# Delaying the side work of the first pass over a dense matrix by four steps: a four-layer graph network kernel on one Trainium2 core

## The chip, the cores and the metric

The kernel runs on one core of a Trainium2 chip (trn2). The metric is device time in microseconds (us) for one execution of the whole program, all four layers; lower is better. Matmuls and transposes run on TensorE (PE in the rows, PEld its weight loads), elementwise work and reductions on VectorE (DVE), activations on ScalarE (ACT), and there are GpSimd (POOL) and the queue of SyncE (SP), which issues most of the transfers.

## The reference

`x` is 8192x128, `adj` a dense 8192x8192 fp32 array that is mostly zeros. Every layer starts from `h = relu(layernorm(x))` and ends in `x = x + layer(h, adj)`.

```
# layer 0: weighted mean over neighbours, then a linear map
x = x + relu((inv_deg[:, None] * A_prime @ h) @ W0.T + b0)     # A_prime = alpha*adj, diagonal + (1-alpha)
# layer 1: a product W1 in hyperbolic space, a mean over adj, and a map back
XW = mobius_matvec(W1, h)
x = x + expmap0(relu(logmap0(... adj @ (gamma * XW) / (adj @ (gamma - 1)) ...)))
# layer 2: maximum over the 32 largest entries of each row of adj
x = x + max over topk(adj, 32) of (h @ W2.T + b2)
# layer 3: as layer 1 with a normalised adj + I, a product W3 and a bias
```

Layer 1 needs, for every row of `x` that layer 0 has finished, the layer norm, the clip, the product with `W1`, several norms, a logarithm and a tanh. This is called the preparation of the next layer below.

## The kernel before

The program is written engine by engine, each with its own loops; semaphores tie them together. Its stages are:

- **The start** (to about 59 us of the trace). `x` is loaded and normalised, and multiplied by `W0` ahead of the sums.
- **The first pass** (about 59 to 1476 us). `adj` is read once from HBM as 256 pieces of 1 MB. A piece is 512 rows by 512 columns; 16 pieces in a row (32 pairs of column tiles) make a group of 512 rows, and there are 16 groups, numbered 0 to 15. Each pair K (two per piece, 512 in all) goes through all engines: TensorE transposes it (`turn_pair`, L655) and multiplies the pair before it into the sums (`add_pair`, L667); ScalarE copies the transposed pair out of PSUM (`copy_pair`, L903) and makes a mask of the piece (`mask`, L910); GpSimd multiplies the mask by column numbers (L498); VectorE takes the eight largest of each row (L1473), for the top 32 of layer 2. SyncE stores the transposed pair back to HBM (L427) and loads the next piece (L436). ScalarE has four buffers for copies, which a stored pair frees (L902 waits), and a ring of three pieces of masks: `mask(K)` waits until VectorE has scanned pair K-6.
- **The turned pass** (about 1477 to 2465 us) reads the transposed matrix for layer 1 (L751), with the gathers of layer 2 beside it.
- **The rest** is layer 3, a second reading of the transposed matrix (L783), and the ends of all rows.

**The side work.** When a group's sums are complete, VectorE finishes its rows of `x` (`update`, L1360 to L1374) and sorts its candidates (`pick`, L1269 to L1354). Both are Python generators: VectorE's loop calls `next` on them twice after each piece, one call being a step, so that their instructions are spread between the scans. The preparation of the next layer is a third generator, on ScalarE and on VectorE (`prepare` on each), started at groups 3, 6, 9 and 12 for the three groups of rows before (`PREPS`), and once more behind the pass for the last four groups. ScalarE's generator makes one step per pair, VectorE's two per piece. So step s of both falls on pair s counted from the group at which the preparation began; step 32 is the first of the next group, step 95 the last of the third.

The preparation's handovers, in order:

1. VectorE centres the rows (L1389 at step 5; L1391 and L1392 at step 6) and tells ScalarE (`tell_act`, a semaphore). ScalarE waits for that at step 10 (`pause(10)`, then `wait_job`), squares two tiles per step (L929, six steps), and takes roots (L939).
2. VectorE waits for the roots at step 19, clips and scales (L1396, L1397). ScalarE waits for that at step 25 and squares again, one tile per step. TensorE turns a unit of four tiles at steps 26, 38 and 50 (L679), ScalarE copies it (L950), TensorE multiplies it by `W1` five steps after each turn (L687), and VectorE copies the product out at steps 32, 44 and 56 (L1404).
3. ScalarE squares the products (step 69), takes roots (L962, step 75), a logarithm (step 82) and a tanh (step 90); VectorE works on the small results at steps 77, 84, 85, 92 and 93. The last two are L1438 to L1444 and L1446 to L1449.

`pause(n)` yields n times. A waiting engine waits with everything behind it in its own order: if ScalarE waits in `wait_job`, the copies of the next pairs stand behind it, and TensorE needs them.

At a group's start SyncE holds the load of the group's fifth piece until VectorE has scanned the first pair of the group (L435), and the stores of the group's next pairs stand behind it in its queue:

```
                    if (n - SLOTS) % NPC == 0:
                        sp.wait_ge(scanned, 2 * (n - SLOTS) + 1)
                sp.dma_start(pieces[n % SLOTS], ...)
```

Of the kernel before, what the change touches and what calls it, by code (L numbers as in the profile page):

```python
# [75 lines left out]
def build(nc, x, adj, alpha, w0, b0, w1, w2, b2, w3, b3, out):  # L76
# [5 lines left out]
    NP = NT // 2  # L82
# [8 lines left out]
    LATE = 6  # L91
    PREPS = [(0, 3), (3, 6), (6, 9), (9, 12), (12, 16)]
    UNIT_GAP = 12
    EARLY = 6
    PARTS = [(0, 3), (3, 6), (6, 8)]
    DONE = [(0, 16), (16, 32), (32, 48), (48, 56), (56, 64)]
# [22 lines left out]
    with ctx:  # L119
# [267 lines left out]
        def pause(count):  # L387
            for _ in range(count):
                yield
# [221 lines left out]
        def _(pe):  # L611
# [79 lines left out]
            def adjacency_pass():  # L691
                pe.wait_ge(h0_copied, NG)
                turn_pair(0)
                pe.wait_ge(h0_taken, NG)
                for K in range(PAIRS):
                    if K + 1 < PAIRS:
                        turn_pair(K + 1)
                    add_pair(K)
                    for b, (first, end) in enumerate(PREPS[:-1]):
                        turned_from = end * NP + 20 + 2 * (end - first)  # L700
                        for u in range(first, end):
                            if K == turned_from + UNIT_GAP * (u - first):
                                turn_h1(u, b)
                            if K == turned_from + UNIT_GAP * (u - first) + 5:
                                project_h1(u, b)
# [96 lines left out]
            def turn_out(u):  # L802
                pe.wait_ge(out_scaled, u // SGG + 1)
                if u < EARLY:
                    into = psX[:, :]
# [9 lines left out]
            def project_out(u):  # L815
                pe.wait_ge(pj_copied, 2 * UNITS + u + 1)
                into = psY[:, :] if u < EARLY else halves[u % 2]
                if u < EARLY:
                    pe.wait_ge(out_taken, u)
                elif u >= EARLY + 2:  # L820
                    pe.wait_ge(out_taken, u - 1)
# [5 lines left out]
            def last_chunk():  # L827
                i, par = CHUNKS // 2 - 1, 1
                pe.wait_ge(tiles_made, CHUNKS * CT)
                for s in range(NSG):  # L830
                    pe.wait_ge(sums_added, (CHUNKS - 1) * NSG + s + 1)
                    for kk in range(2):
# [4 lines left out]
                        if turn >= 0:  # L837
                            turn_out(turn)
                project_out(EARLY - 1)
                turn_out(EARLY)  # L840
                for u in range(EARLY, NG):
# [13 lines left out]
        def _(act):  # L855
# [3 lines left out]
            def wait_job():  # L859
                asked[0] += 1  # L860
                act.wait_ge(for_act, asked[0])

            def job(out, in_, func, **kw):
                wait_job()
                nc.scalar.activation(out, in_, func, **kw).then_inc(from_act, 1)
# [58 lines left out]
            def prepare(first, end):  # L924
                tiles = range(first * TPG, end * TPG)
                ts = slice(first * TPG, end * TPG)

                def square(row, t):
                    st.mark(nc.scalar.activation(junk_tile, G[:, t, :], ACT.Square, accum_out=sm[:, row, t:t + 1]))  # L929
                    st.settle()  # L930

                yield from pause(10)
                wait_job()
                for t in tiles:
                    square(0, t)
                    if t % 2:
                        yield
                st.settle()
                nc.scalar.activation(sm[:, 1, ts], sm[:, 0, ts], ACT.Sqrt, scale=1.0 / P, bias=eps_col[:, :])\  # L939
                    .then_inc(from_act, 1)  # L940
                yield from pause(9)
                wait_job()
                for t in tiles:
                    square(2, t)
                    if t % TPG == TPG - 1:
                        u = t // TPG
                        act.wait_ge(pj_turned, u + 1)
                        if u >= 2:
                            act.wait_ge(pj_out, u - 1)
                        nc.scalar.activation(HT[:, u % 2, :], psX[:, :], ACT.Copy).then_inc(pj_copied, 1)  # L950
                        if end < NG:
                            yield from pause(UNIT_GAP - TPG)
                    yield
                st.settle(tell=from_act)
                yield from pause(8)
                wait_job()
                for t in tiles:
                    square(3, t)
                    if t % 2:
                        yield  # L960
                st.settle()
                nc.scalar.activation(sm[:, 7:9, ts], sm[:, 2:4, ts], ACT.Sqrt).then_inc(from_act, 1)  # L962
                yield from pause(7)
                job(sm[:, 13, ts], sm[:, 12, ts], ACT.Ln)
                yield from pause(8)
                job(sm[:, 5, ts], sm[:, 5, ts], ACT.Tanh)
# [212 lines left out]
        def _(dve):  # L1179
# [197 lines left out]
            def prepare(first, end):  # L1377
                ts = slice(first * TPG, end * TPG)
                n = (end - first) * TPG
# [11 lines left out]
                link(v.tensor_scalar(T(0), T(0), -1.0 / P, None, ALU.mult))  # L1391
                link(v.tensor_tensor(G[:, ts, :], X[:, ts, :], by_row(T(0), n), ALU.add))  # L1392
                tell_act()
                yield from pause(n // 2 + 7)
                answered()
                link(v.reciprocal(T(1), U(1)))  # L1396
                link(v.scalar_tensor_tensor(G[:, ts, :], G[:, ts, :], 0.0, by_row(T(1), n), ALU.max, ALU.mult),  # L1397
# [4 lines left out]
                for u in range(first, end):  # L1402
                    dve.wait_ge(pj_out, u + 1)
                    v.tensor_copy(G[:, u * TPG:(u + 1) * TPG, :], ps[:, :].rearrange("p (r f) -> p r f", f=P))\  # L1404
                        .then_inc(pj_taken, 1)
                    yield from pause(UNIT_GAP if u + 1 < end else 4)
                answered()
                dve.wait_ge(pj_taken, end)
                tell_act()
                yield from pause(n // 2 + 11)  # L1410
                answered()
                y, ys, q, y2, m = T(5), U(1), T(11), U(10), U(9)
                link(v.tensor_scalar(rows[:, 2:4, :], sm[:, 7:9, ts], 1e-15, None, ALU.max))
# [670 lines left out]
```

## Time and profile before

| what | value |
|---|---|
| time, median of 3 runs | 3695.63 us (3692.3 to 3698.97) |
| span of the profiled execution | 3738.5 us |
| first pass, from the first to the last product | 59 to 1476 us |
| TensorE busy | 3378.0 us, 90% of the span |
| VectorE busy | 2622.0 us, 70% |
| GpSimd busy | 2592.6 us, 69% |
| ScalarE busy | 1607.0 us, 43% |
| mean granted TensorE clock | 0.963 |

The page gives for the profiled execution its span only, no time of its own; the span is 42.9 us above the median of the timed runs. Columns of a timeline row are the start, the time to the end of the merged run of instructions, engine, line, operation, output<-input, shapes, how many, and in brackets the idle time of the engine before it with what ended it.

### The profile page before, as it was taken

The page shows a single profiled execution, that of the slowest core. Times are in us where ns is not written, and L with a number is a line of the kernel's source. Part 1 is how long each engine was busy: PE and PEld are TensorE (multiplying, and loading weights), DVE is VectorE, ACT ScalarE, POOL GpSimd, SP SyncE. Part 2 cuts the span into 40 slices and gives each one's busy share as a digit, 9 for nine tenths or more (in the row PEclk, how much of TensorE's full clock was granted, in tenths as well). Part 3 has the DMA queues.
Part 4 walks back from the last instruction along what each step waited for, and adds up shares of the span by engine and source line. Part 5 has one row for each costly group of instructions (what it writes and reads, how often), then busy time and mean ns, then how long its engine had stood idle before and what let it go on. Part 6 is the DMA issues. An engine that isn't in the chain of part 4 may idle for free.

```text
span 3738.5 us, 76487 instructions
## 1 busy us (share of the span) xinstructions
PE 3378.0 (90%) x29444; PEld 3342.4 (89%) x29444; DVE 2622.0 (70%) x5491; ACT 1607.0 (43%) x3554; POOL 2592.6 (69%) x2448
## 2 busy tenths in 40 slices
PE   6999999999999999999999999942899898989894
PEld 6999999999999999999999999942888898989894
DVE  6788888788788788211177664647787878878767
ACT  6777887787787786222122211221111111112114
POOL 3998998998998997000487856647888878777500
PEclk9999999999999999999999999975999999999997
DMA  6999999999999999788888888842788887878781
GB/s 217 397 396 367 388 385 352 386 389 352 386 391 351 384 376 388 276 291 296 290 322 319 299 294 311 293 154 77 269 286 291 300 308 284 295 280 308 259 293 57
DMA packets 401324, 1155.22 MB, mean 309 GB/s; under 512 B 36717, under 2 KB 56110, under 8 KB 401006
## 3 DMA queue, kind: packets, MB, share of 16 engines
q1 hardware_dynamic: 360096, 1082.21, 78.4%
q0 software_dynamic: 31360, 64.29, 5.5%
q10 hardware_dynamic: 9550, 4.69, 0.4%
q8 instruction: 174, 2.85, 0.3%
q14 instruction: 144, 1.18, 0.1%
HBM read 874.19 MB, written 276.86 MB: 308 GB/s over the span
## 4 chain that ended last, share of the span: by engine, by line
PE 65%; DVE 21%; issue 5%; POOL 4%; ACT 2%; DMA 1%; another core or an unknown queue 1%; DVEq 1%; POOLq 0%; SPq 0%; ACTq 0%
PE psU L667 18%; PE psT L751 18%; PE psT L655 9%; PE psT L783 8%; PE psU L751 6%; DVE agg L1684 4%; DVE HT L1680 3%; PE psU L783 3%; DVE D L1473 2%; POOL D L498 2%; POOL D L506 2%; DVE GR L1843 1%; DVE W L1684 1%; DMA adj_turned<-ATS 1%
## 5 line engine op out<-in xcount | busy, mean ns | idle before, releaser
L498 POOL TENSOR_TENSOR D<-D,iota 128x512 f32<-128x512 f32 x1024 | 1307.3, 1307 | 115.9 <-ACT D L910 97.6
L667 PE MATMUL psU<-HB,ATS 128*128 128x129 f32 x8192 | 1007.1, 276 | 28.4 <-ACT ATS L903 26.3
L667 PEld LDWEIGHTS psU<-HB,ATS 128*128 128x128 f32 x8192 | 961.1, 193 | 33.3 <-ACT ATS L903 28.6
L783 PE MATMUL psT<-ATS,PIECES 128*128 128x129 f32 x6144 | 804.7, 281 | 172.7 <-ACT ATS L1069 79.3
L783 PEld LDWEIGHTS psT<-ATS,PIECES 128*128 128x128 f32 x6144 | 751.5, 196 | 186.3 <-issue 143.8
L1473 DVE MAX8 D<-D 128x8 f32<-128x512 f32 x1024 | 644.2, 683 | 259.7 <-POOL D L498 251.9
L751 PE MATMUL psT<-GR,PIECES 128*128 128x129 f32 x6144 | 780.7, 276 | 20.1 <-issue 19.3
L751 PEld LDWEIGHTS psT<-GR,PIECES 128*128 128x128 f32 x6144 | 733.2, 192 | 24.9 <-issue 24.2
L506 POOL DMA_INDIRECT D<-h_table,idx_own x624 | 628.4, 1007 | 170.4 <-issue 150.3
L903 ACT ACTIVATE ATS<-psT 128x512 f32<-128x512 f32 x1024 | 555.9, 596 | 270.4 <-PE psT L655 177.1
L910 ACT ACTIVATE D<-PIECES 128x1024 f32<-128x1024 f32 x512 | 544.1, 1063 | 0.0
L655 PE MATMUL psT<-ident,PIECES 128*128 128x128 f32 x4096 | 530.7, 273 | 0.0
L655 PEld LDWEIGHTS psT<-ident,PIECES 128*128 128x128 f32 x4096 | 465.1, 142 | 0.1
L751 PE MATMUL psU<-GR,PIECES 128*128 128x129 f32 x2048 | 317.3, 276 | 11.3 <-issue 11.2
L783 PE MATMUL psU<-ATS,PIECES 128*128 128x129 f32 x2048 | 320.3, 279 | 3.2 <-issue 3.0
L517 POOL TENSOR_TENSOR D<-D 128x512 bf16<-128x512 bf16 x212 | 222.8, 1051 | 117.4 <-DVEq L60 103.2
L751 PEld LDWEIGHTS psU<-GR,PIECES 128*128 128x128 f32 x2048 | 272.0, 192 | 14.5 <-issue 14.4
L783 PEld LDWEIGHTS psU<-ATS,PIECES 128*128 128x128 f32 x2048 | 276.4, 196 | 4.9 <-issue 4.8
L1053 ACT ACTIVATE junk_rows<-X 128x128 f32<-128x128 f32 x64 | 19.8, 309 | 569.0 <-DVE X L1717 334.8
L506 POOL DMA_INDIRECT D<-h_table,idx_pool x215 | 211.2, 983 | 71.8 <-issue 53.3
L1843 DVE TENSOR_TENSOR GR<-psT,GR 128x387 f32<-128x387 f32 x240 | 122.5, 552 | 138.0 <-PE psU L783 102.3
L1684 DVE TENSOR_REDUCE agg<-HT 128x128 f32<-128x896 f32 (+2 forms) x120 | 187.4, 1562 | 4.1
(410 smaller groups left out, 2896.9 us busy)
## 6 DMA issues: line engine op xcount, KB each, us to landing
PIECES<-adj_turned SPq DMA_DIRECT2D x512, 1024.0 KB
PIECES<-in_adj SPq DMA_DIRECT2D x256, 1024.0 KB
adj_turned<-ATS SPq DMA_DIRECT2D x512, 512.0 KB, 8.2
D<-h_table,idx_own POOLq DMA_INDIRECT x624
h_table<-HB ACTq DMA_DIRECT2D x8, 512.0 KB, 6.6
D<-h_table,idx_pool POOLq DMA_INDIRECT x215
out_x<-X SPq DMA_DIRECT2D x3, 1024.0 KB, 5.1
ATS<-h_table,idx_pool POOLq DMA_INDIRECT x117
```

Source lines behind the costliest of these rows:

```text
L498: pool.tensor_tensor(key, key, iota[:, :], ALU.mult).then_inc(keyed, 1)
L506: pool.indirect_dma_start(slot, None, rows, bass.IndirectOffsetOnAxis(ap=index, axis=0)).then_inc(done, inc)
L517: pool.tensor_tensor(idle, idle, idle, ALU.add).then_inc(rested, 1)
L655: last = nc.tensor.transpose(psT[h][:, b * GROUP + r * P:b * GROUP + (r + 1) * P], pieces[n % SLOTS][:, r, x0:x0 + P], ident[:, :])
L667: last = nc.tensor.matmul(sum4(r), AT[K % NAT][:, b * GROUP + r * P:b * GROUP + (r + 1) * P], HB[:, j, :], start=(j == 0 and r % 2 == 0), ...
L751: last = nc.tensor.matmul(acc(s % 2, r), block_of(q % SLOTS, b, r), GR[:, j, :], start=(j == 0 and opens(r)), stop=(j == NT - 1 and closes ...
L783: last = nc.tensor.matmul(acc(h, r), block_of(slot, b, r), Hc[par][:, jj, :], start=(jj == 0 and opens(r)), stop=(jj == CT - 1 and closes(r)))
L903: nc.scalar.activation(AT[K % NAT][:, half], psT[K % 2][:, half], ACT.Copy).then_inc(pair_copied, 1)
L910: nc.scalar.activation(KEY[n % NKEY][:, rows, :], pieces[n % SLOTS][:, rows, :], ACT.Sign)\
L1473: last = v.max(cand[g % 2][:, c, r, :], KEY[n % NKEY][:, r, :])
L1684: v.tensor_reduce(part_max[k], kept[:, 0:size, :].rearrange("p k f -> p f k"), AX.X, ALU.max)\
L1843: last = v.tensor_tensor(sums, acc_rows(m % 2, n), sums, ALU.add)
```

## The change

It adds a constant `BEHIND = 4` and puts it into pauses:

```
-                        turned_from = end * NP + 20 + 2 * (end - first)
+                        turned_from = end * NP + 21 + BEHIND + 2 * (end - first)
...
-                yield from pause(10)
+                yield from pause(10 + BEHIND)
                 wait_job()
...
                 tell_act()
-                yield from pause(n // 2 + 7)
+                yield from pause(n // 2 + 7 + BEHIND)
                 answered()
...
                 tell_act()
-                yield from pause(n // 2 + 11)
+                yield from pause(n // 2 + 9)
                 answered()
```

The first is on TensorE (its turns and products of units come five steps later: turns at 31, 43, 55, products at 36, 48, 60), the second on ScalarE (everything of it four steps later: 14, 29, 73, 79, 86, 94), the last two on VectorE. VectorE's centring stays at steps 5 and 6; its clip goes from step 19 to 23, its copies from 32, 44, 56 to 36, 48, 60, and its later work from 77, 84, 85, 92, 93 to 79, 86, 87, 94, 95. No instruction is added or taken away. GpSimd's and SyncE's orders are the same. The line numbers of the changed kernel are one higher than before in what follows the constant.

Three places of the order of instructions show it. **First**, ScalarE at group 3, where the first preparation's squares begin (L929, L930 in the changed kernel); before:

```order
L903 ACTIVATE ATS<-psT 128x512 x2
L910 ACTIVATE D<-PIECES 128x1024
L903 ACTIVATE ATS<-psT 128x512 x2
L910 ACTIVATE D<-PIECES 128x1024
L929 ACTIVATE junk_rows,sm<-GR 128x128 x2
L903 ACTIVATE ATS<-psT 128x512 x2
L910 ACTIVATE D<-PIECES 128x1024
L929 ACTIVATE junk_rows,sm<-GR 128x128 x2
L903 ACTIVATE ATS<-psT 128x512 x2
L910 ACTIVATE D<-PIECES 128x1024
```

and changed:

```order
L904 ACTIVATE ATS<-psT 128x512 x2
L911 ACTIVATE D<-PIECES 128x1024
L904 ACTIVATE ATS<-psT 128x512 x2
L911 ACTIVATE D<-PIECES 128x1024
L904 ACTIVATE ATS<-psT 128x512 x2
L911 ACTIVATE D<-PIECES 128x1024
L904 ACTIVATE ATS<-psT 128x512 x2
L911 ACTIVATE D<-PIECES 128x1024
L930 ACTIVATE junk_rows,sm<-GR 128x128 x2
L904 ACTIVATE ATS<-psT 128x512 x2
L911 ACTIVATE D<-PIECES 128x1024
L930 ACTIVATE junk_rows,sm<-GR 128x128 x2
```

The first pair of squares stood behind the eleventh mask of the group (row numbers are left out here); it now stands behind the fifteenth.

**Second**, VectorE where the first preparation ends and group 6 begins: the last step of the preparation (L1446 to L1449), the scans of a piece (L1473), the first instructions of the next group's sorting (L1269, L1270), and the look at the new group's first piece (L1467, L1468). Before:

```order
L1446 RECIPROCAL psY<-psY 128x12
L1447 TENSOR_SCALAR GR<-psY 128x12
L1448 SCALAR_TENSOR_TENSOR psY<-psY,sm 128x12
L1449 TENSOR_TENSOR GR<-GR,psY 128x12x128
L1473 MAX D<-D 128x8 x4
L1269 SCALAR_TENSOR_TENSOR D<-D 128x64 x4
L1270 TENSOR_SCALAR psY<-psY 128x4
L1467 TENSOR_SCALAR D<-PIECES 128x256
L1468 TENSOR_REDUCE psY<-PIECES 128x4
L1473 MAX D<-D 128x8 x4
```

and changed, where the scans are L1474:

```order
L1447 RECIPROCAL psY<-psY 128x12
L1448 TENSOR_SCALAR GR<-psY 128x12
L1449 SCALAR_TENSOR_TENSOR psY<-psY,sm 128x12
L1450 TENSOR_TENSOR GR<-GR,psY 128x12x128
L1270 SCALAR_TENSOR_TENSOR D<-D 128x64 x4
L1271 TENSOR_SCALAR psY<-psY 128x4
L1468 TENSOR_SCALAR D<-PIECES 128x256
L1469 TENSOR_REDUCE psY<-PIECES 128x4
L1474 MAX D<-D 128x8 x4
```

The four scans that stood between the last instruction of the preparation and the new group's first instruction now stand ahead of the preparation's last two steps. The same holds at groups 9 and 12, and at group 15 for the fourth preparation.

**Third**, VectorE at group 4, the copy of the first product (L1404, L1405 in the changed kernel), before with the group's first two pieces of scans:

```order
L1473 MAX D<-D 128x8 x4
L1273 TENSOR_TENSOR D<-D,psY 128x512
L1275 TENSOR_SCALAR own<-psY 128x4
L1277 TENSOR_SCALAR D<-D 128x512
L1404 COPY GR<-psX 128x4x128
L1280 TENSOR_REDUCE psY<-D 128x4
L1281 TENSOR_TENSOR D<-D 128x512
L1473 MAX D<-D 128x8 x4
```

and changed, with the scans of the third piece ahead of it:

```order
L1294 TENSOR_SCALAR psY<-psY 128x4
L1372 TENSOR_TENSOR agg<-agg,psY 128x512
L1373 TENSOR_TENSOR agg<-agg,bias 128x512
L1474 MAX D<-D 128x8 x4
L1297 TENSOR_SCALAR D<-D 128x512
L1300 MAX D<-D 128x8 x4
L1375 SCALAR_TENSOR_TENSOR X<-agg,X 128x512
L1405 COPY GR<-psX 128x4x128
L1300 MAX D<-D 128x8 x4
L1474 MAX D<-D 128x8 x4
```

The copy stood behind the scans of the group's first piece; it now stands behind those of the third and behind the whole update of `x` (L1375 is its last instruction).

## Rows read from the trace of the kernel before

**Rows 1.** Windows: stretch, length; busy PE, PEld, DVE, ACT, POOL; clock, DMA, GB/s.
```profile
60.00:1474.00 1414.00, 1385.57 (x12393) 1380.67 (x12393) 1136.93 (x2545) 1112.75 (x1921) 1304.63 (x1022) 0.99 1.00 379
...
1474.00:1561.00 87.00, 85.90 (x770) 85.74 (x769) 40.14 (x134) 28.69 (x113) 2.70 (x3) 1.00 0.81 283
```

**Rows 2.** Waits in the first pass: who <- whom: total us, times, longest.
```profile
ACT junk_rows L929 <- DVEq L1190: 27.1, 4, 7.6
...
SPq L435 <- DVE D L1473: 61.0, 16, 5.4
```

**Rows 3.** Timeline of TensorE: products of pairs around step 10, groups 3, 6, 9, 12.
```profile
342.55 1.95 PE L667 MATMUL psU<-HB,ATS 128*128 128x129 f32 x16
...
354.73 1.95 PE L667 MATMUL psU<-HB,ATS 128*128 128x129 f32 x16
...
357.39 1.95 PE L667 MATMUL psU<-HB,ATS 128*128 128x129 f32 x16
...
610.47 1.95 PE L667 MATMUL psU<-HB,ATS 128*128 128x129 f32 x16
...
623.99 1.95 PE L667 MATMUL psU<-HB,ATS 128*128 128x129 f32 x16
...
880.05 1.95 PE L667 MATMUL psU<-HB,ATS 128*128 128x129 f32 x16
...
893.75 1.95 PE L667 MATMUL psU<-HB,ATS 128*128 128x129 f32 x16
...
1149.09 1.95 PE L667 MATMUL psU<-HB,ATS 128*128 128x129 f32 x16
...
1159.34 3.53 PE L667 MATMUL psU<-HB,ATS 128*128 128x129 f32 x16 [7.42 <-ACT ATS L903]
...
1163.58 1.95 PE L667 MATMUL psU<-HB,ATS 128*128 128x129 f32 x16
```

**Rows 4.** Windows: the granted clock around the stall of group 12.
```profile
1155.50:1163.00 7.50, 3.67 (x19) 3.67 (x20) 7.15 (x23) 5.05 (x14) 2.21 (x2) 0.54 0.42 127
```

**Rows 5.** Timeline of ScalarE in group 12: steps 4 and 8, then the stall.
```profile
1129.97 1.09 ACT L903 ACTIVATE ATS<-psT 128x512 f32<-128x512 f32 x2 [0.63 <-PE psT L655]
1130.94 1.06 ACT L910 ACTIVATE D<-PIECES 128x1024 f32<-128x1024 f32 x1
...
1143.02 1.09 ACT L903 ACTIVATE ATS<-psT 128x512 f32<-128x512 f32 x2 [1.96 <-DMA adj_turned<-ATS]
...
1157.82 0.31 ACT L929 ACTIVATE junk_rows<-GR 128x128 f32<-128x128 f32 x1 [7.62 <-DVEq L1190]
...
1158.68 1.08 ACT L903 ACTIVATE ATS<-psT 128x512 f32<-128x512 f32 x2
...
1161.47 1.09 ACT L903 ACTIVATE ATS<-psT 128x512 f32<-128x512 f32 x2
```

**Rows 6.** Timeline of TensorE in group 12: the product of pair 4.
```profile
1132.79 1.95 PE L667 MATMUL psU<-HB,ATS 128*128 128x129 f32 x16
```

**Rows 7.** Timeline of VectorE in group 12: the scans of pairs 8 and 9.
```profile
1158.91 2.47 DVE L1473 MAX8 D<-D 128x8 f32<-128x512 f32 x4
```

**Rows 8.** Timeline of ScalarE in group 6: ahead of the roots, step 16.
```profile
634.80 1.28 ACT L939 ACT_TABLE_LOAD   x1
```

**Rows 9.** Timeline of VectorE: the first preparation's end, group 5, with a scan behind it.
```profile
578.15 0.22 DVE L1438 RECIPROCAL psY<-psY 128x12 f32<-128x12 f32 x1
...
582.27 2.47 DVE L1473 MAX8 D<-D 128x8 f32<-128x512 f32 x4
```

**Rows 10.** One line of VectorE's sorting in the pass: min/median/max duration in ns.
```profile
L1316 DVE CAST POOLN<-D x15: 435/994/4218, 186.8 to 1435.4; 128x12 uint16<-128x12 f32 x15
```

**Rows 11.** Timelines at group 4: TensorE's second turn (step 38); VectorE's third and fourth piece.
```profile
427.03 0.60 PE L679 MATMUL psX<-ident,GR 128*128 128x128 f32 x4
...
430.79 2.47 DVE L1473 MAX8 D<-D 128x8 f32<-128x512 f32 x4
...
436.19 2.47 DVE L1473 MAX8 D<-D 128x8 f32<-128x512 f32 x4
```

More of the change, by code:

```diff
@@ L93, in build @@
     UNIT_GAP = 12
+    BEHIND = 4
     EARLY = 6
```

## The prediction

> **What bounds the kernel now.** I read the windows first. In the first pass TensorE is busy for 1385.6 of 1414 us at nearly the full clock, more than any other engine [rows 1]; GpSimd is next with 1304.6 and VectorE has 1136.9. So a microsecond in which TensorE does nothing there is a microsecond of the program, and the work of the others counts only where TensorE comes to wait for it. The reader is to see the same in the timeline of TensorE: the products of one pair follow those of the pair before by 357.39 - 354.73 = 2.66 us [rows 3], and 512 pairs at that rate are 1362 us of the pass. What is above it is side work of TensorE and stalls.
>
> The waits then say where the stalls are. ScalarE waited 27.1 us in four places for VectorE at the squares of L929, up to 7.6 us each [rows 2]. These are step 10 of the four preparations: ScalarE asks for centred rows that VectorE has not finished, and the copies that TensorE needs stand behind the wait. The timeline of TensorE prices it: between the pair before the stall and the second pair behind it lie two periods, 5.32 us, if nothing stalls. In group 3 it took 354.73 - 342.55 = 12.18, in group 6 13.52, in group 9 13.70 and in group 12 14.49 [rows 3]. The excess is 6.9 + 8.2 + 8.4 + 9.2 = **32.6 us**. A part of it is the clock: TensorE ran the first pair behind the gap at a granted 0.54 of full speed over the stretch [rows 4], that is mostly at 1.2 GHz, after 7.42 us without work [rows 3].
>
> **The change, part by part.**
>
> *The wait at step 10, now at 14: takes 32.6 us away.* Four steps are 4 x 2.66 = 10.6 us, the longest wait is 7.62 [rows 5], and VectorE's centring is not moved. It is ready 3 us before ScalarE asks in group 12, and more in the others. The whole excess goes, the half clock with it.
>
> *VectorE's last two steps of a preparation, from 92 and 93 to 94 and 95: gives about 10.4 us back.* Step 93 fell behind the 47th piece's scans, so one piece of scans stood between it and the next group. Steps 94 and 95 fall behind the 48th, the last piece. They take 582.27 - 578.15 = 4.1 us with what lies between [rows 9]. Before, these 4.1 us were followed by scans that ended at 584.7. In the new order the scans come first, at the earliest two periods after the ones that ended at 578.15, so at 583.5 or, as GpSimd's small backlog shrinks, 583.1; then the 4.1 us. The new group's sorting starts at 587.2 to 587.6 in place of 584.7. I take 2.6 us later. VectorE's first scan of the group is later by as much, and SyncE is already waiting for just that (L435: 16 waits, up to 5.4 us [rows 2]), with the stores of the next pairs queued behind the load. ScalarE's copies wait for those stores: in group 12 the copy of pair 8 began at 1143.02 after 1.96 us of waiting for one [rows 5], where four periods after 1129.97 would be 1140.61, so 2.4 us late. What TensorE can bear is its lead: a product began 1132.79 - 1129.97 = 2.82 us after its copy normally [rows 5, 6] and 1159.34 - 1158.68 = 0.66 at the least [rows 3, 5], so 2.16 us. It is used up already, and each further microsecond of lateness is a stall. This holds where a preparation has just ended: groups 6, 9, 12 and 15. 4 x 2.6 = 10.4. The lower bound is nothing (if the stores land early enough), the upper 4 x 4.1 = 16.4.
>
> *ScalarE's squares meet VectorE's backlog: gives about 4.8 us back.* The stall also let VectorE catch up. Without it `mask(K)` meets the scan of pair K-6. In group 12 pair 8's scan ended halfway through 2.47 us from 1158.91, at 1160.15 [rows 7]; mask 14 without delay would start ten periods after 1130.94, at 1157.54 [rows 5], so it is 2.6 us late. From the mask to the next copy it is 0.97 less than 2.66 normally, 1.69, and with two squares between 0.95 + 0.87 = 1.82; the copy is 2.7 late and TensorE loses 2.7 - 2.16 = 0.55. Each further step with squares takes 1161.47 - 1158.68 = 2.79 [rows 5], 0.13 over the period: five make 0.65. Then the roots bring a table load of 1.28 us [rows 8] and 0.3 for themselves, against 2.66 - (2.79 - 0.87) = 0.74 that a step without squares leaves: 0.85. Group 12: 2.1. Groups 6 and 9, whose stalls were about 0.9 shorter, I put at 1.4 and 1.3, group 3, 2.3 shorter and with the table of the roots still loaded, at nothing: 4.8. The lateness of the item before does not come on top, for a stall of TensorE moves pairs and deadlines alike. Bounds: 0, and 9 if all four cost what group 12 does.
>
> *TensorE's turns and products, five steps later: nothing.* They are the same instructions on the engine that sets the end, wherever they stand. Their cover is margin in steps: the clip is at 23, the turn at 31 (before, 19 and 26); ScalarE's copy of the turned unit at 32 follows the turn by one step where it was two, still behind a copy, a mask and a square, 2.4 us of its own. The waits of ScalarE at 29, 73, 86 and 94 keep or gain distance to VectorE's 23, 64, 79 and 87. Pieces of GpSimd and SyncE are not moved past anything.
>
> *The last preparation, behind the pass: nothing.* VectorE's longer pauses there only call a sorting generator that has ended. TensorE was busy for 85.9 of the 87 us that follow the pass [rows 1], so no handover held it. What the pass gains therefore arrives at the end of the program: all that follows hangs on TensorE's sums.
>
> **Sum.** -32.6 + 10.4 + 4.8 = -17.4 us. The sum is of one profiled execution with a span of 3738.5; the timed median is 42.9 lower, so some of the waits may be shorter there. I subtract it from the median: 3695.63 - 17.4 = **3678 us**. Changes of less than 0.2% (7.4 us) can't be told from none.
>
> **A rule that speaks against it.** One line of VectorE's sorting shows how a small instruction can wait there: a cast of 12 columns took 435 ns at least, 994 in the median and 4218 once [rows 10]. That once was group 2, with GpSimd running without a gap. The stalls gave GpSimd gaps in the very steps; the change closes them. The Trainium skill, "SBUF — State Buffer", section "Who interferes with whom", says that VectorE's casts and copies in their fast modes and GpSimd lock one shared port pair against each other for whole instructions. The trace agrees with the direction. As a mechanism: in the four preparing groups the cast takes 4.2 in place of 1.0, and VectorE is 3.2 us later from then on.
>
> **The rivals.**
>
> *A, the forecast* (0.46): 3678, between 3669 and 3687 by the bounds above taken together.
>
> *B, the group's start costs nothing* (0.17): SyncE's later load is absorbed. For: the lateness rests on one landing time. Against: TensorE has no lead left there. -32.6 + 4.8: 3668.
>
> *C, the clock falls in the new stalls* (0.13): a gap of 2.6 us and more at four group starts lets the clock go to 1.2 GHz. A pair behind the gap took 1163.58 - 1159.34 = 4.24, 1.6 over the period [rows 3]. For: the same engine at the same work. Against: the gaps are half as long. 3678 + 6.4: 3685.
>
> *D, GpSimd blocks the casts* (0.08): 3.2 us in four groups, of which the scans' slack takes a part: 3680 to 3691, I take 3686.
>
> *E, the timed executions have only half of the stalls* (0.09): VectorE is faster when not profiled. The span is 42.9 above the median and that lies somewhere. -16.3 + 7.6: 3687.
>
> *F, slower* (0.07): TensorE comes to wait for VectorE's copy of a product. The copy is at step 36, behind the scans of the group's third piece and the whole update of `x`; the second turn at 43 needs the same PSUM bank. In group 4 those scans ended at 433.26 and the next began at 436.19, so with the copy it is done by 436.9; the turn, five periods behind 427.03, is due at 440.3 [rows 11]. The margin is 3.4 us. From there on every microsecond of VectorE stalls TensorE, in four groups. To lose, it would have to be 3.4 + (17.4 + 7.4) / 4 = 9.6 us later than I read; as all of it holds up the other queues, 3705. Against it: nothing in group 4 grows by so much.
>
> **How the numbers follow.** The range takes A, B, C, D and half of E, with the 3 us by which single runs lie beside the median: 3661 to 3690. Faster by over 0.2% (below 3688.2) hold A, B, C, most of D and half of E: 0.85. Within 0.2% what is left of D and E: 0.08. Slower: F, 0.07.
>
> **What the changed profile would show.** Right: no wait of ScalarE for VectorE at the first squares; TensorE's two periods around step 10 at 5.3 us and no half clock there; SyncE's longest wait at the group's start near 8 us; TensorE idle for some 3 us about steps 6 to 9 of groups 6, 9, 12 and 15; small gaps of ScalarE for VectorE's scans at step 14 of groups 6, 9 and 12. Wrong: a new wait of 5 us or more of ScalarE or of TensorE anywhere in the pass, or a pass shortened by less than 10 us or by more than 28.

## The result, and the profile after

The changed kernel takes 3687.23 us (median of 20 runs, 3679.94 to 3697.01), the kernel before beside it on the same chip 3694.07 (20 runs, 3688.01 to 3705.19): a ratio of 0.9983 with an interval of 0.9975 to 0.9990. That is 6.8 us less, 0.2%, where I had forecast 17.4 less. The time is inside my range (3661 to 3690). The later runs found the kernel before at 3673 us, 20 us less than here, so in all that follows a ratio is taken against the kernel before of the same comparison.

The first lines of the changed kernel's page:

```profile
span 3678.2 us, 76487 instructions
...
PE 3363.6 (91%) x29444; PEld 3338.7 (91%) x29444; DVE 2618.0 (71%) x5491; ACT 1608.0 (44%) x3554; POOL 2596.3 (71%) x2448
```

The span is 60 us under that of the profile before, 3738.5. This is not the gain. From the first product of pair 0 to the first of pair 511 the first pass took 1415.0 us before (59.16 to 1474.17 in TensorE's timeline) and takes 1410.3 now (60.63 to 1470.95): 4.7 us. What lies behind it took 2264.3 and now 2207.2, and in the seven other kernels of this study and in a second profile of the changed one it took 2191.1 to 2203.9, three of these being the kernel before with an edit inside the pass only. The profile before stands alone with its 2264.3, and 57 us of the difference between the spans are that.

So the question is the pass. The waits in it, of the changed kernel (who <- whom: total us, times, longest):

```profile
ACT ATS L904 <- PE psT L656: 160.3, 255, 1.5
...
ACT ATS L904 <- DMA adj_turned<-ATS: 120.9, 82, 8.2
...
PE psU L668 <- ACT ATS L904: 20.1, 4, 5.3
...
ACT D L911 <- DVE D L1474: 2.2, 2, 1.9
...
SPq L436 <- DVE D L1474: 78.8, 16, 10.4
```

The 27.1 us of ScalarE at the squares [rows 2] are gone. In their place TensorE waits four times for ScalarE's copies, 5.3 us at the longest, ScalarE up to 8.2 us for a store to land, and SyncE up to 10.4 us for VectorE's first scans of a group, where it was 5.4 [rows 2]. The same four waits in TensorE's timeline, at group 6:

```profile
589.40 1.95 PE L668 MATMUL psU<-HB,ATS 128*128 128x129 f32 x16
592.07 1.95 PE L668 MATMUL psU<-HB,ATS 128*128 128x129 f32 x16
600.10 3.81 PE L668 MATMUL psU<-HB,ATS 128*128 128x129 f32 x16 [5.21 <-ACT ATS L904]
```

Pair 4, pair 5, then 8.03 us to pair 6, whose product itself takes 3.81 us rather than 1.95. The windows around it (busy PE, PEld, DVE, ACT, POOL; clock, DMA, GB/s) show why:

```profile
599.00:603.50 4.50, 3.40 (x16) 3.40 (x17) 4.26 (x10) 3.95 (x6) 1.95 (x2) 0.50 1.04 406
```

The granted clock is 0.50, the lower level, 1.2 GHz, right behind 5.21 us without work.

How it comes about, in the order of the queues. ScalarE at group 6: the mask of pair 4, the mask of pair 5, then the copy of pair 6.

```profile
587.56 1.06 ACT L911 ACTIVATE D<-PIECES 128x1024 f32<-128x1024 f32 x1
...
590.22 1.06 ACT L911 ACTIVATE D<-PIECES 128x1024 f32<-128x1024 f32 x1
599.45 1.09 ACT L904 ACTIVATE ATS<-psT 128x512 f32<-128x512 f32 x2 [8.17 <-DMA adj_turned<-ATS]
```

SyncE's queue there:

```profile
590.44 0.38 SPq L437 DMA_DIRECT2D PIECES<-in_adj  x1
590.87 0.98 SPq L428 DMA_DIRECT2D adj_turned<-ATS  x2
```

The load at 590.44 waited for VectorE's scans of the group's first pair, and the two stores behind it could only then be issued. The first of them is the store of pair 2, whose buffer the copy of pair 6 needs. These stores land 8.2 us after their issue in the median of the page, and the copy of pair 6 begins 8.6 us after it, at 599.45. The load is issued 590.44 - 587.56 = 2.9 us after the mask of pair 4. In the profile before it was issued 2.2 us ahead of that mask:

```profile
589.76 0.38 SPq L436 DMA_DIRECT2D PIECES<-in_adj  x1
...
591.92 1.06 ACT L910 ACTIVATE D<-PIECES 128x1024 f32<-128x1024 f32 x1
```

The first line is SyncE's, the second ScalarE's mask of pair 4, of the kernel before. **VectorE is 5.0 us later at a group's start where I had put 2.6.** It is the same in groups 9, 12 and 15, where it is 5.3, 5.3 and 5.0 later. I call this number, the end of those scans against the mask's time carried back by four periods, the group-start lateness: 5.3 to 7.3 us in an ordinary group of these two kernels, 8.1 to 8.4 before in these four, 13.4 now.

The whole pass can be added up in this way: for each pair the time to the next pair's product less the period of 2.66 us, summed over all sixteen groups by the pair's place in its group. (The rest, 1.1 to 1.4 us at pairs 0 to 3 of most kernels, 5.1 in the one with three steps, is left out; some 10 us at pairs 22 to 31 stand in every kernel.) Each row is one profiled execution. The two of the changed kernel differ by 1.2 us in the pass and by up to 1.3 in a column, so smaller differences between rows are not read as effects.

| kernel | pass | pairs 4-8 | 9-11 | 12-21 | 22-31 |
|---|---|---|---|---|---|
| before | 1415.0 | 4.3 | 36.3 | 1.7 | 11.8 |
| changed | 1410.3 | 33.1 | 1.7 | 4.6 | 10.0 |
| changed, second time | 1411.5 | 34.4 | 1.8 | 3.6 | 10.6 |
| ending put back | 1395.3 | 6.2 | 2.2 | 14.2 | 11.7 |
| only the ending late | 1431.0 | 23.1 | 26.0 | 8.4 | 12.6 |
| the same, tanh late too | 1436.3 | 32.1 | 28.7 | 2.1 | 12.6 |
| only the squares moved | 1394.1 | 4.6 | 3.9 | 12.5 | 12.2 |
| a store ahead of the load | 1407.3 | 21.3 | 1.8 | 11.6 | 11.5 |
| ending back and store ahead | 1399.7 | 5.1 | 2.9 | 20.5 | 10.2 |
| three steps, ending back | 1392.5 | 2.1 | 2.4 | 10.9 | 12.3 |

Between the first two rows: -34.6 + 28.8 + 2.9 - 1.8 = -4.7 us, the whole change of the pass.

### The profile page after: what moved, and what is told of

Its sections match the earlier page's. It is cut to its first block, busy times and chain, and to the rows that moved or that the text cites. A ratio compares the mean times of both kernels' runs of the same rounds, so it can differ in the third digit from the quotient of the medians.

```text
span 3678.2 us, 76487 instructions
## 1 busy us (share of the span) xinstructions
PE 3363.6 (91%) x29444; PEld 3338.7 (91%) x29444; DVE 2618.0 (71%) x5491; ACT 1608.0 (44%) x3554; POOL 2596.3 (71%) x2448
## 4 chain that ended last, share of the span: by engine, by line
PE 73%; DVE 15%; issue 6%; POOL 3%; ACT 2%; DMA 1%; DVEq 1%; SPq 0%; POOLq 0%; ACTq 0%
PE psU L668 23%; PE psT L752 16%; PE psT L656 11%; PE psT L784 11%; PE psU L752 5%; PE psU L784 4%; DVE agg L1685 3%; DVE HT L1681 2%; POOL D L507 2%; DVE GR L1844 1%; DVE W L1685 1%; DMA adj_turned<-ATS 1%; DVE agg L1690 1%; POOL D L518 0%; POOL D L499 0%
## 5 line engine op out<-in xcount | busy, mean ns | idle before, releaser
L1474 DVE MAX8 D<-D 128x8 f32<-128x512 f32 x1024 | 644.0, 683 | 254.4 <-POOL D L499 247.0
L752 PEld LDWEIGHTS psT<-GR,PIECES 128*128 128x128 f32 x6144 | 730.3, 192 | 10.6 <-issue 10.2
```

The lines of the kernel that those rows point to most:

```text
L752: last = nc.tensor.matmul(acc(s % 2, r), block_of(q % SLOTS, b, r), GR[:, j, :], start=(j == 0 and opens(r)), stop=(j == NT - 1 and closes ...
L1474: last = v.max(cand[g % 2][:, c, r, :], KEY[n % NKEY][:, r, :])
```

## The experiments

Theory G said that the preparation's last steps, now behind the last piece's scans, make the group start late, and that this costs the missing microseconds. The rivals were that the moved squares and turns themselves cost them, that SyncE's order of queue is what makes the lateness dear, and, for the 2.4 us per group that my reading had missed, that something else besides the order of VectorE is behind them.

**1. The ending put back.** The change, with the whole last part of ScalarE and VectorE (steps 69 to 93) where it was:

```diff
-                            yield from pause(UNIT_GAP - TPG)
+                            yield from pause(UNIT_GAP - TPG - (BEHIND if t == tiles[-1] else 0))
...
-                    yield from pause(UNIT_GAP if u + 1 < end else 4)
+                    yield from pause(UNIT_GAP if u + 1 < end else 2)
```

> The changed kernel, with its last part put back where it was before: ScalarE's pause behind the last copied unit is four steps shorter, VectorE's behind the last product two, so that roots, logarithm, tanh and VectorE's steps stand at 69 to 93 again; the squares still begin at step 14. Theory G (group start): the four new stalls at pairs 5 and 6 of groups 6, 9, 12 and 15 (7.6, 8.5, 7.1 and 6.3 us of TensorE) come from VectorE's last two steps behind the last piece, which hold up SyncE's stores. They then shrink to what was there before, under 1 us each, no pair of the pass but the boundaries takes over 4 us, and the time is some 27 us below the changed kernel, about 3660. Rival B (backlog): they come from VectorE never catching up once the stall at step 10 is gone; then they stay, and the time is 3687. Rival L (lost later): the pass gets shorter by 27 us, and the time doesn't.

It measured 3648.55 us against 3673.52 before: 0.9939 (0.9923 to 0.9956), the change alone having 0.9983. By the ratios that is some 16 us less than the change, not 27. The pass is 15 us shorter than in the changed kernel, 26.9 us of stalls at pairs 4 to 8 are gone and 9.6 come back at 12 to 21. In group 6, 1.6 us of stall stay at pairs 4 to 8, where I had expected under 1; in the other three it is 0.2 to 0.6. The stalls do not stay as they were and the time follows the pass, so rivals B and L are out. Its waits:

```profile
ACT ATS L904 <- DMA adj_turned<-ATS: 91.7, 76, 3.7
...
ACT D L911 <- DVE D L1474: 5.6, 3, 3.0
PE psU L668 <- ACT ATS L904: 9.0, 10, 2.3
...
SPq L436 <- DVE D L1474: 59.9, 16, 6.5
```

SyncE's longest wait is down to 6.5, ScalarE's for a store to 3.7. G holds for the group's start. Most of what comes back is the backlog term of my sum, here at group 12 in TensorE's timeline:

```profile
1151.28 2.05 PE L668 MATMUL psU<-HB,ATS 128*128 128x129 f32 x16 [2.33 <-ACT ATS L904]
1154.07 2.05 PE L668 MATMUL psU<-HB,ATS 128*128 128x129 f32 x16
```

A gap of 2.33 us, then pairs 2.79 apart: the mask ahead of the squares of step 14 waited 2.96 us for VectorE's scan. The clock did not fall here: the granted clock is 1.00 from 1150 to 1155 us, and the product takes 2.05 us. Another 2.2 us of the 14.2 at pairs 12 to 21 are in group 5, where ScalarE's logarithm waited 3.5 us for VectorE.

**2. Only the ending late.** The kernel before with VectorE's last part two steps later (79, 86, 87, 94 and 95), and nothing else:

```diff
-                yield from pause(n // 2 + 11)
+                yield from pause(n // 2 + 13)
```

> The kernel before with one pause of VectorE two steps longer, so that only its last part moves, to steps 79, 86, 87, 94 and 95; ScalarE and TensorE stay. Theory G: the stalls at pairs 5 and 6 of groups 6, 9, 12 and 15 appear, 6 to 8 us each, beside the four at step 10, of which three get some 3 us shorter since VectorE catches up in the new ones: about 3713, between 3708 and 3721. Rival B: nothing new at pairs 5 and 6, 3694.

3686.73 us, ratio 1.0041 (1.0023 to 1.0059): 13 to 15 us slower than the kernel before, at the low end of what I expected (3708 to 3721 against 3694, that is 14 to 27 more). The stalls at pairs 4 to 8 appear (18.8 us more), with 26.0 of the 36.3 us at pairs 9 to 11 still there. So the ending alone does it. The 8.4 us at pairs 12 to 21 hold a side effect that the change does not have: ScalarE's logarithm, still at step 82, waits for VectorE's step 79, 7.5 us in all, and 5.0 us of stall in group 11 go with it. But the group-start lateness is 14.9, 12.2, 10.8 and 10.8 us in groups 6, 9, 12 and 15, not 13.4 each. In the last two it is 2.7 and 2.4 us above the 8.1 and 8.4 of the kernel before, about the 2.6 that I had read out of the order of instructions. For these two groups something that was in the change and is not here brings the other 2.6. Groups 6 and 9 are late by more than that without it, group 6 by more than in the change itself: VectorE's last scans of the old group end 3.0 us after the mark there (the mask's time carried back) and 1.8 to 1.9 in groups 12 and 15. What held them up in those two groups was not traced.

**3. A store ahead of the load.** The changed kernel, in SyncE's order of the pass: the stores behind the load of each group's first piece are issued ahead of it.

```diff
                 if n >= SLOTS:
-                    store_pairs(n - SLOTS)
+                    if not (n - SLOTS > 1 and (n - SLOTS) % NPC == 1):
+                        store_pairs(n - SLOTS)
+                    if n - SLOTS and (n - SLOTS) % NPC == 0:
+                        store_pairs(n - SLOTS + 1)
```

> The changed kernel with one thing of SyncE's order changed: at a group's fifth piece the stores of the next two pairs are issued ahead of the wait for VectorE's first scan, not behind it. VectorE's lateness stays. Theory G with SyncE's queue as the link: ScalarE no longer waits for a stored pair at pair 6, the four stalls go to under 2 us each, and the time is 3658 to 3666. If the late load is what holds TensorE, or VectorE itself through the ring of masks, a stall of 3 us or more stays in each of the four groups and the time is above 3670. Rival B: 3687.

3663.74 us, ratio 0.9973 (0.9963 to 0.9984), where 3658 to 3666 against 3694 would have been 0.990 to 0.992. The interval overlaps that of the change alone (0.9975 to 0.9990), so the gain over it rests on the pass, 1407.3 us and 3.0 shorter. The stalls moved by two pairs, from ahead of pair 6 to ahead of pair 8, and shrank from 29.6 us to 5.2 + 3.7 + 5.3 + 3.4 = 17.6. So a stall of over 3 us stayed in each of the four groups, which I had named as the sign that the late load or VectorE itself holds TensorE. At group 6, SyncE, ScalarE's copy of pair 8, and TensorE's products of pairs 7 and 8:

```profile
588.63 0.94 SPq L440 DMA_DIRECT2D PIECES<-in_adj  x2
589.63 1.25 SPq L428 DMA_DIRECT2D adj_turned<-ATS  x2
...
601.00 1.09 ACT L907 ACTIVATE ATS<-psT 128x512 f32<-128x512 f32 x2 [6.20 <-DMA adj_turned<-ATS]
...
595.58 1.95 PE L671 MATMUL psU<-HB,ATS 128*128 128x129 f32 x16
601.65 3.50 PE L671 MATMUL psU<-HB,ATS 128*128 128x129 f32 x16 [3.24 <-ACT ATS L907]
```

The copy of pair 8 waits for a store, and that store, of pair 4, stands behind the late load. TensorE waited for loads 0.5 us in the whole pass, so it is not the load that holds it. The stall follows the stores that stand behind the waiting load, whichever they are: a piece brings two pairs, so moving one piece's stores moves the stall by two pairs. I had the link right and the size wrong: the copy begins 11.4 us after this store's issue, behind two loads, where it was 8.6 behind one in the changed kernel, so of the 5.3 us that two periods give, 2.8 are lost again. VectorE's lateness is untouched (13.4 in all four groups).

**4. Both.** Experiment 1 with SyncE's edit of experiment 3.

```diff
-                            yield from pause(UNIT_GAP - TPG)
+                            yield from pause(UNIT_GAP - TPG - (BEHIND if t == tiles[-1] else 0))
...
-                    yield from pause(UNIT_GAP if u + 1 < end else 4)
+                    yield from pause(UNIT_GAP if u + 1 < end else 2)
...
-                    store_pairs(n - SLOTS)
+                    if not (n - SLOTS > 1 and (n - SLOTS) % NPC == 1):
+                        store_pairs(n - SLOTS)
+                    if n - SLOTS and (n - SLOTS) % NPC == 0:
+                        store_pairs(n - SLOTS + 1)
```

> The last part put back and the stores ahead of the wait, both on the changed kernel. Theory G: about as the better of the two, with the small stalls of the kernel before at pairs 6 to 8 (2.0 us in all) gone as well: 3655 to 3662. If it is as slow as the worse one, the two edits have a cost of their own.

3653.81 us, ratio 0.9953 (0.9938 to 0.9969). It is not better than experiment 1 (0.9939, intervals overlap), and less than the 3655 to 3662 against 3694 (0.989 to 0.991) that I had expected. The stalls at 4 to 8 lose another 1.1 us and those at 12 to 21 gain 6.3. In group 3 VectorE's scans of pair 8 end 2.6 us later (against the masks) than in experiment 1, and the squares meet that. Why an earlier store makes VectorE later I did not follow up.

**5. The change once more**, with no edit, beside the next three.

> The changed kernel, unedited, beside the others of this call and its own runs of the kernel before. Theory G: the ratio to the kernel before is again 0.998, the first pass some 5 us shorter than before (1410 against 1415 us from the first to the last product), and the stretch behind the pass differs from execution to execution by more than that.

3665.02 us (12 runs) against 3672.8 (19 runs): 0.9979 (0.9968 to 0.9990), that is 7.8 us less. The group-start lateness is 13.44 in three of the groups and 13.43 in the fourth, as in the first profile. The gain of 7 to 8 us and its make-up are reproduced.

**6. Three steps in place of four, the ending put back.** Experiment 1 with

```diff
-    BEHIND = 4
+    BEHIND = 3
```

> The version with the last part put back, with all of the delay three steps in place of four (squares at 13, VectorE's clip at 22, TensorE's turns at 30, 42, 54). Three steps are 8.0 us, the longest of the four waits was 7.62 and VectorE's centring is some 1 us later there in the version put back: theory G expects ScalarE to wait for VectorE at the squares again for up to 1 us in groups 9 and 12, at no cost beyond TensorE's lead, and a time within 4 us of the version with four steps. If ScalarE's wait returns with 3 us or more, the delay needed is set by something else than the wait of the kernel before.

3643.65 us (3636.66 to 3647.2), ratio 0.9913 (0.9897 to 0.9929): 29 to 32 us faster than before. It is the lowest time of all, but its interval overlaps those of experiments 1 and 8. Its waits:

```profile
ACT junk_rows L930 <- DVEq L1191: 6.0, 4, 2.5
...
PE psU L668 <- ACT ATS L904: 5.0, 10, 1.5
```

ScalarE waits for VectorE's centring again, 6.0 us in all and more than I had expected, but TensorE loses only 5.0 in the whole pass. VectorE's last steps stand one step earlier than before and the lateness at groups 6, 9, 12 and 15 is 6.8 to 6.9 us, that of an ordinary group. The stalls at 12 to 21 are 3.3 us less than in experiment 1.

**7. The tanh late too.** Experiment 2 with ScalarE's tanh at step 94, where the change has it, in place of 90:

```diff
-                yield from pause(8)
+                yield from pause(12)
```

> The kernel before with VectorE's last part two steps later (as in e2_end_late) and, on ScalarE, only the tanh moved from step 90 to 94, beside the end of the group. In e2_end_late VectorE's first scan of the group ended 10.8 us behind the mark in groups 12 and 15, in the changed kernel 13.4 in all four. Theory T: the rest of the lateness is ScalarE's tanh with its table load of 1.28 us, which delays the masks of the group's last pair; then it is 13.4 here too, and TensorE loses at pairs 5 and 6 of group 15 some 6 us where e2_end_late lost 2.6. Rival: it is VectorE's own instructions that take longer beside GpSimd; then it stays at 10.8.

3694.86 us, ratio 1.0057 (1.0040 to 1.0075), an interval that overlaps that of experiment 2; the difference is in the trace. The group-start lateness is 13.4 us in all four groups and group 15 stalls by 7.8 us where experiment 2 had 2.8. In groups 12 and 15 this is what was missing. In group 6 the lateness is less than in experiment 2 (13.4 and 14.9), so a late tanh is not the only way to it. How it acts is to be seen at group 12. VectorE and GpSimd with the tanh at 90 (experiment 2):

```profile
1133.38 1.29 DVE L1473 MAX8 D<-D 128x8 f32<-128x512 f32 x2 [1.19 <-POOL D L498]
...
1138.71 2.07 DVE L1269 TENSOR_TENSOR_SCAN D<-D 128x64 f32<-128x64 f32 x4
...
1136.52 2.53 POOL L498 TENSOR_TENSOR D<-D,iota 128x512 f32<-128x512 f32 x2 [0.26 <-ACT D L910]
1139.29 8.04 POOL L498 TENSOR_TENSOR D<-D,iota 128x512 f32<-128x512 f32 x6 [0.24 <-ACT D L910]
```

and with the tanh at 94 (this kernel), ScalarE's load of the tanh's table first:

```profile
1125.85 1.28 ACT L865 ACT_TABLE_LOAD   x1
...
1131.90 1.29 DVE L1473 MAX8 D<-D 128x8 f32<-128x512 f32 x2 [2.16 <-POOL D L498]
...
1137.23 3.86 DVE L1269 TENSOR_TENSOR_SCAN D<-D 128x64 f32<-128x64 f32 x4
...
1137.00 9.26 POOL L498 TENSOR_TENSOR D<-D,iota 128x512 f32<-128x512 f32 x7 [0.19 <-ACT D L910]
```

The tanh and its table load hold ScalarE's masks up two pairs before the group ends, in place of six. GpSimd, which needs the masks, falls behind, VectorE waits 2.16 us instead of 1.19 for it ahead of the group's last scans, and GpSimd then works on without a gap (7 instructions in 9.26 us) where it had one within VectorE's four small sorting scans before. Those scans take 3.86 us in place of 2.07. That the tanh with its table load moved the start of groups 12 and 15 is shown by this pair of kernels, which differ in nothing else. That the slower scans are GpSimd's doing is read from the rows, whose spans of GpSimd are rough, and was not tried by itself.

The Trainium skill, "SBUF — State Buffer", section "Who interferes with whom", says that a VectorE instruction with two inputs in SBUF contends with a GpSimd instruction that reads SBUF, and that the contention is an exclusive lock. The trace agrees in kind: the same four instructions at 2.07 us beside a gap of GpSimd, 3.86 without one. It does not show that the gap decides: in the kernel before they took 2.96 us at group 6, with GpSimd idle for 0.4 us beside them.

**8. Only the squares moved.** The kernel before with ScalarE's squares four steps later and VectorE's clip two, and all of the rest, turns and ending too, where it was:

```diff
-                yield from pause(10)
+                yield from pause(14)
...
-                yield from pause(9)
+                yield from pause(5)
...
-                yield from pause(n // 2 + 7)
+                yield from pause(n // 2 + 9)
...
-                yield from pause(13)
+                yield from pause(11)
```

> The smallest form of the change: on the kernel before, ScalarE's first squares at step 14 and its second still at 25, VectorE's clip at 21, all else (TensorE's turns, VectorE's copies, the whole last part) where it was. Theory G: the stalls at step 10 go, none come at the group's start; VectorE's clip at 21 is ready some 12 us behind the mark and ScalarE asks 11.6 behind it, so waits of up to 1 us at step 25 in groups 9 and 12: a time within 4 us of the version with the last part put back. If the handover of the clip becomes the bound, TensorE stalls at step 26 by 2 us or more in each group and the time is over 10 us above that version.

3649.47 us, ratio 0.9934 (0.9915 to 0.9952), as experiment 1. The useful part of the change is the squares' four steps, with the clip's two. The 12.5 us at pairs 12 to 21 are there too, so the turns' new place is not their cause.

## Why the prediction missed, step by step

- *The squares' wait, -32.6.* Right. The time of pairs 9 to 11 fell by 34.6 us, and 1.9 of it only changed its place with the turns of groups 4, 7, 10 and 13, coming back at 12 to 31. There is no wait of ScalarE for VectorE's centring left in the pass, and experiment 8 gets the gain from this edit alone.
- *The later start of groups 6, 9, 12 and 15, +10.4.* **This step failed.** The mechanism was right, the queue included: VectorE's ending behind the 48th piece, SyncE's load waiting for it, stores behind the load, ScalarE's copy, TensorE. The sum was 4 x 2.6 and it came to 27.5 (29.6 less the 2.0 which the same pairs of these groups already lost before). The term was mis-sized in two places: VectorE was 5.0 to 5.3 us late, not 2.6, and the half clock behind the stalls, which I had only as rival C, cost 8.8 more. Three things made it so. First, I left the tanh out. I had written that the waits of ScalarE at 94 "keep or gain distance" and never asked what the instructions of that step would hold up at the group's end; the 1.28 us of its table load are my own [rows 8]. Second, VectorE's instructions there are not of fixed length:

```profile
578.28 1.29 DVE L1474 MAX8 D<-D 128x8 f32<-128x512 f32 x2 [2.15 <-POOL D L499]
...
583.61 3.85 DVE L1270 TENSOR_TENSOR_SCAN D<-D 128x64 f32<-128x64 f32 x4
587.56 1.13 DVE L1468 TENSOR_SCALAR D<-PIECES 128x256 f32<-128x256 f32 x1
```

  of the changed kernel, against these of the kernel before at the same place:

```profile
584.66 2.96 DVE L1269 TENSOR_TENSOR_SCAN D<-D 128x64 f32<-128x64 f32 x4
587.73 0.29 DVE L1467 TENSOR_SCALAR D<-PIECES 128x256 f32<-128x256 f32 x1
```

  That is 0.9 and 0.8 us more. Set against the mask of pair 4 (587.56 here, 591.92 before), the first of these scans starts 3.3 us later, 0.7 more than my 2.6, since the group's last scans wait longer for GpSimd. Together 2.6 + 0.7 + 0.9 + 0.8 = 5.0, as measured. Group 15 is like group 6. In groups 9 and 12 the small scans took 3.85 us where it was 1.85 before, and the TENSOR_SCALAR 1.1 both times: 2.6 + 0.7 + 2.0 = 5.3. Third, the clock. From pair 5 to pair 6 it takes 5.4, 5.5, 5.2 and 4.8 us over the period, 20.8 in all, and the pairs behind add 2.3, 3.0, 1.9 and 1.5, 8.8 in all; the first product behind each gap took 3.81, 3.81, 3.81 and 3.47 us. 20.8 + 8.8 less the 2.0 of before is the 27.5, but for rounding.
- *The squares against VectorE's backlog, +4.8.* In the change itself it came to 1.0 (group 3), for the stall at the group's start gives VectorE the time that the later one would have taken; I had said that the two add up and they don't. Where that stall is gone it is larger than I put it: 8.4 us at pairs 12 to 21 of groups 3, 6, 9 and 12 in experiment 1, 6.3 with three steps, against 4.8. Step 14 in group 12 lost 2.5 us (experiment 1) where I had 0.55, where VectorE's scans of pair 8 ended 2.0 us later than in the profile before.
- *Turns, products, and the last preparation, nothing.* Right within what is measured: TensorE waited for none of VectorE's copies in the pass, and experiment 8, which leaves the turns alone, gains no more than experiment 1, which moves them. Behind the pass nothing is slower.
- *The rivals.* B, a free start of the group, is out (experiments 1 and 2). C, the clock, happened in all four places. I had its price about right (6.4, it was 8.8). Whether the gaps of 2.6 us that I forecast would have brought it, the runs leave open. Of nine gaps between 2.2 and 3.15 us in the passes of all the profiles, three were followed by a slow product (2.25 us in group 12 of experiment 2, with 3.05) and six were not (2.33 in experiment 1, and 2.98 and 3.12 in groups 15 and 9 of experiment 3, with 2.05 each). All 27 gaps of 3.15 us and more were, so with the gaps of 5 us that came it belonged in the sum. D, casts held up by GpSimd: in the pass the cast of 12 columns took 0.91 us in the median and 6.6 once, in group 2 again, with 0.99 and 4.2 before [rows 10], so not in its form; its reason, GpSimd without gaps, fits the scans above. E, half of the stalls in timed runs: the pass's 4.7 us and the runs' 6.8 and 7.8 agree to 3.1 us, and nothing speaks for it. F: no wait of TensorE for VectorE.

Altogether: -32.6 + 27.5 + 1.0 - 0.7 (small stalls of group 7, gone) = -4.8, and the pass is 4.7 shorter. "A new wait of 5 us or more of ScalarE or of TensorE anywhere in the pass" was what I had named as a sign of being wrong, and it was there, four times; the other sign, a pass shortened by less than 10 us, was there too.

## What to carry to other kernels

When a block of work is moved by a few steps, look at its tail as well as at its head: where the last of it lands in the order of every engine decides what starts late, and a later head with the tail where it was gained 22 to 32 us here (experiments 1, 6 and 8), head and tail moved together 7. Follow the late instruction into queues that are served in order: a load that waits takes the stores behind it along. And a lateness that TensorE can just bear is not to be priced at its own size: beyond that margin each further microsecond cost one here, and the gaps of 3.2 us and more also cost the clock of the pair behind them.

## What the runs showed of the hardware

- Gaps of TensorE of 3.24 and 5.21 us were followed by a product at 3.50 and 3.81 us in place of 1.95, the granted clock 0.50 in the window around the second; after 2.33 us it was 2.05, at 1.00. The length of the gap alone does not decide between these: 2.25 us was followed by 3.05 (experiment 2), 3.12 by 2.05 (experiment 3, clock 1.00).
- Four identical small scans of VectorE took 1.9 us at most group starts and 3.85 at the four late ones of the changed kernel, where each of them took either 0.26 or 1.2 to 1.3 us. GpSimd was idle for 0.4 us beside the first and 0.06 beside the second, but 2.96 us came with 0.4 idle as well. A TENSOR_SCALAR over 256 columns took 0.29 or 1.1 to 1.3 us.
- The copy that waited for a 512 KB store began 8.6 us after the store's issue where one load had been issued just ahead of it (group 6 of the changed kernel), and 11.4 us where two had (group 6 of experiment 3).
- One profiled execution lay 57 to 73 us above the others in stages that no edit touched, while its first pass was like the rest. Had the spans been compared, the change would have looked like a gain of 60 us.
